# The mask additions of one batch moved from VectorE to GpSimd, with every engine's list of work laid out anew

## The reference, cut to what matters

```
h = relu(layernorm(x))
q, k, v = h @ Wq.T + bq, h @ Wk.T + bk, h @ Wv.T + bv         # 4 heads of 32
s = clip(q @ k.T / sqrt(32), -10, 10); s = where(adj == 0, -10, s)
attn = softmax over each of 8 chunks of 128 columns apart
x = x + layernorm(sum over chunks(attn @ v) @ Wo.T + bo + h) * gamma + beta

h = relu(layernorm(x)); Wh = h @ W
e = leaky_relu(Wh @ a1 [row] + Wh @ a2 [column], 0.2)          # 1024 x 1024
e = where(adj > 0 or i == j, e, -inf)
x = x + elu(softmax(e) @ Wh)
```

## Time and profile before

| | |
|---|---|
| median of 3 runs | 709.34 us (707.78 to 710.83) |
| the profiled execution | 708.66 us, its span 706.9 us |
| DVE busy | 662.2 us (94%), 1165 instructions |
| ACT busy | 649.4 us (92%), 1140 |
| PE busy | 647.7 us (92%), 4393 |
| POOL busy | 523.0 us (74%), 629 |

### The profile page before, as it was taken

One profiled execution on the slowest core, in us unless ns is written; L12 is line 12 of the kernel. 1 busy time (PEld: TensorE's weight loads), 2 busy tenths in 40 slices (PEclk: granted clock), 3 DMA queues, 4 the chain that ended last, 5 costly groups with the idle time before them and its releaser, 6 DMA issues. The chain is left out here.

```text
span 706.9 us, 13598 instructions
## 1 busy us (share of the span) xinstructions
PE 647.7 (92%) x4393; PEld 348.3 (49%) x4393; DVE 662.2 (94%) x1165; ACT 649.4 (92%) x1140; POOL 523.0 (74%) x629
## 2 busy tenths in 40 slices
PE   3689999999899999999999999999999999995976
PEld 1433443343355554547455554556436463564865
DVE  1899999999999999999999999999999999999875
ACT  2799999998999999999999989999999989997665
POOL 2144585663779888898889768988879778889864
PEclk9999999999999999999999999999999999998899
DMA  8742133224211233233223143122232213010111
GB/s 285 245 155 105 68 128 120 96 83 150 90 52 62 98 120 120 84 112 109 72 76 125 63 150 112 60 76 105 83 112 98 69 46 106 16 46 30 54 52 47
DMA packets 58647, 68.53 MB, mean 97 GB/s; under 512 B 5328, under 2 KB 35024, under 8 KB 58576
## 3 DMA queue, kind: packets, MB, share of 16 engines
q1 hardware_dynamic: 57568, 67.39, 28.1%
q10 hardware_dynamic: 1008, 0.26, 0.2%
HBM read 21.50 MB, written 12.58 MB: 48 GB/s over the span
## 5 line engine op out<-in xcount | busy, mean ns | idle before, releaser
L1452 DVE SCALAR_TENSOR_TENSOR probs<-score,cap 128x1024 f32<-128x1024 f32 x256 | 305.5, 1212 | 5.6 <-ACT score L1297 4.4
L1297 ACT ACTIVATE score<-score 128x1024 f32<-128x1024 f32 x256 | 259.9, 1028 | 10.7 <-PE score L1644 9.9
L1644 PE MATMUL score<-query_stack,key_stack 128*128 128x512 f32 x512 | 186.4, 451 | 18.9 <-DVE probs L1452 17.2
L1224 POOL TENSOR_TENSOR gathered<-gathered,scaled 128x512 f32<-128x512 f32 x112 | 154.4, 1379 | 53.5 <-DVE scaled L1478 52.6
L1249 POOL TENSOR_TENSOR ring<-ring,see_t 128x512 f32<-128x512 f32 x112 | 133.1, 1200 | 17.7 <-DVE ring L1543 17.5
L1644 PEld LDWEIGHTS score<-query_stack,key_stack 128*128 128x128 f32 x512 | 79.5, 189 | 131.8 <-DVE probs L1452 100.4
L1661 PE MATMUL work<-probs,ones 128*32 128x512 f32 x1024 | 135.2, 602 | 0.1
L1655 PE MATMUL work<-probs,value 128*32 128x512 f32 x1024 | 132.8, 598 | 0.1
L1727 PEld LDWEIGHTS work<-wh,ring 128*128 128x128 f32 x896 | 107.2, 194 | 17.8 <-issue 7.6
L1727 PE MATMUL work<-wh,ring 128*128 128x130 f32 x896 | 110.5, 280 | 4.4 <-ACT ring L1365 4.3
L1365 ACT ACTIVATE ring<-ring,wh 128x512 f32<-128x512 f32 x128 | 90.2, 735 | 5.9 <-POOL ring L1249 3.9
(11 more groups left out here) (117 smaller groups left out, 836.8 us busy)
## 6 DMA issues: line engine op xcount, KB each, us to landing
query_stack<-parts SPq DMA_DIRECT2D x64, 256.0 KB, 2.9
key_stack<-parts SPq DMA_DIRECT2D x56, 256.0 KB, 2.5
x_in<-in_x SPq DMA_DIRECT2D x16, 256.0 KB, 2.9
h_kept<-x_in SPq DMA_DIRECT2D x16, 256.0 KB, 2.2
res<-h_kept SPq DMA_DIRECT2D x16, 256.0 KB, 2.7
h<-in_x SPq DMA_DIRECT2D x16, 256.0 KB, 3.2
x_kept<-res SPq DMA_DIRECT2D x16, 256.0 KB, 2.2
gat_x<-x_kept SPq DMA_DIRECT2D x32, 128.0 KB, 2.2
```

Source lines behind the costliest of these rows:

```text
L1224: nc.gpsimd.tensor_tensor(sums, sums, scaled[:, k % SCALED], ALU.add).then_inc(gathered_step, 1)
L1297: nc.scalar.activation(some, some, ACT.Exp, scale=DH ** -0.5).then_inc(exp_done, 1)
L1452: nc.vector.scalar_tensor_tensor(out=probs[:, group_of(b, k) % KEPT], in0=score[:, h:h + GROUP, :], scalar=LOW, in1=caps.broadcast_to([P, ...
L1644: last = nc.tensor.matmul(score[:, head, :], key_stack[:, head, chunk * P:(chunk + 1) * P], query_stack[:, head, half * HALF:(half + 1) * ...
```

## The change

In the table VECTOR, batch 6 loses its eight `hide` steps (the odd tiles); in GPSIMD all sixteen have a place. Batch 7 keeps half and half, batches 0 to 5 were POOL's before and stay so. All five tables and BANKS have new numbers throughout. The code that walks them is untouched; its lines stand five lower in the new file, since a table became shorter.

```diff
 VECTOR = {
     0: {
...
-        "bias_row": [1092],
...
+        "bias_row": [2829],
...
     6: {
...
-        "hide": [None, 4986, None, 5120, None, 5253, None, 5386, None, 5714, None, 6120, None, 6188, None, 6256],
...
 GPSIMD = {
...
     6: {
...
-        "hide": [4818, None, 4933, None, 5047, None, 5162, None, 5566, None, 5915, None, 6112, None, 6226],
...
+        "hide": [5500, 5614, 5875, 6119, 6234, 6348, 6463, 6577, 6692, 6991, 7106, 7220, 7335, 7449, 7564, 7678],
...
 SYNC = {
     0: {
...
-        "store_h": [920, 1992],
-        "load_residual": [1190, 2365],
...
+        "store_h": [1250, 2320],
...
+        "load_residual": [2225, 5283],
```

More of the change, by code:

```diff
@@ L49 @@
         "turn_x": [932, 1794],
[L50 to L66, removed]
-    },
-    1: {
[L69 to L83, removed]
-    },
@@ L85 @@
-    2: {
[L86 to L103, removed]
-    },
@@ L105 @@
-    3: {
[L106 to L123, removed]
-    },
@@ L185 @@
[L185 to L203 removed]
+        "mask": [1132, 1284, 1485, 1949, 2027, 2167, 2413, 3230],
@@ new lines @@
+        "see": [1130, 1236, 1326, 1858, 2100, 2134, 7222, 7796],
+        "cast": [1164, 1370, 2040, 2464],
+        "key": [1430, 2963],
+        "edges": [1496, 1710, 1892, 2168, 2316, 3635, 5033, 5407],
+        "query": [1644, 3283],
+        "probs": [2525, 2638, 2850, 3057, 3170, 3409, 3522, 3783, 3896, 4147, 4366, 4480, 4718, 4920, 5181, 5294,
+            5615, 5728, 5979, 6152, 6353, 6484, 6717, 6908, 7109, 7256, 7435, 7683, 7830, 8026, 8276, 8418],
+        "bias_row": [2829],
+        "gather": [3349, 4010, 4593, 4832, 5555, 5842, 6092, 6265, 6597, 7021, 7548, 7943, 8139, 8597, 8770, 9286],
@@ L680 @@
[L680 to L693 removed]
+        "beta": [2630, 8343],
@@ new lines @@
+    3: {
+        "rstd_x": [-19410, -18182],
+        "gather": [None, -4158, -4016, -3213, -2795, -2650, -1812, -1569, None, 223, 365, 608, 977, 1434, 1679,
+            2257],
+        "residual": [-1326, 2664],
+        "beta": [1220, 2385],
+        "rstd_y": [2072, 6671],
+        "gamma": [2517, 7341],
+        "x1": [2984, 7501],
+        "rstd_z": [4291, 7990],
+        "row_shift": [12157],
+        "hide": [12998, 13113, 13227, 13342, 13468, 13847, 14306, 14549, 15109, 15245, 15917, 16530, 16773, 16980,
+            17095, 17605],
+        "add_x1": [15707, 17523, 19536, 19649],
+        "add_below": [16887, 19038, 19731, 23336],
+    },
@@ new lines @@
+    7: {
+        "rstd_x": [-23736, -21191],
+        "gather": [None, -10590, -10448, -10052, -9445, -9202, -8866, -8605, None, -7690, -7203, -6786, -6314,
+            -5661, -5315, -4818],
+        "residual": [-9695, -5532],
+        "beta": [-8738, -6092],
+        "rstd_y": [-5846, -4285],
+        "gamma": [-5186, -3871],
+        "x1": [-4947, -3610],
+        "rstd_z": [-4470, -2794],
+        "row_shift": [-737],
+        "hide": [-302, None, -170, None, 42, None, 336, None, 467, None, 679, None, 910, None, 1122],
+        "add_x1": [1025, 1334],
+        "add_below": [1237, 1429],
```

1159 lines of the change are left out of this document (593 added, 566 removed).

## The result

The changed kernel takes 703.21 us in the median (702.33 to 704.53, 4 runs), the kernel before 709.33 beside it (707.78 to 710.83, 4 runs). The ratio is 0.9912, with a 95% interval of 0.9895 to 0.993. It is faster by 6.1 us; 704.8 was predicted. The profiled execution took 702.33 us with a span of 700.6, which is 6.3 less than the span of 706.9 before.

A forecast was written before the change was run, and what follows sets the result against it. DVE, ACT and PE together were taken to bound the middle, with open time at both ends. 708.66 - 7.4 (start) - 0.8 (middle) + 4.0 (end) = 704.5 us, or 705.1 from the median; 704.8 was predicted, range 698 to 711.

The forecast's parts named there:

- The start: Up to the first `probs`: bias_row later and stacks issued earlier bring it 7.4 us forward, with 4.6 and 8.9 as ends.
- the end: First leaky of batch 6 to first of batch 7: eight more hides on POOL delay the shares, 4.0 us dearer.
- The middle: From 50 us to the last `probs`: two DVE instructions leave this stretch, 0.8 us won, with 4 us to either side.
- the last stretch: The last 27.1 us, from the first leaky of batch 7: same work, so 0, with 1 us to either side.
- behind the last `probs`: After the last `probs`, DVE busy only 15.77 of 17.88 us: a leaky and an invert of batch 5 cost nothing there.
- the rest of the new order: In the middle: can win at most the 11.5 us of idle time; given 0 with 4 us to either side.
- The peaks of batch 7: In the end: said to finish before the last share, so row_shift still waits for the copies of wh.
- The free end: Rival: the end costs 1 us or nothing; 701.5 us, or 698 if the middle loses 3 us idle; chance 0.25.
- The loads: Rival: stacks crawl behind set-up loads, or mask tiles wait; first `probs` at 30 us, 708.5 us, no change; chance 0.17.
- The stalled middle: Rival: new lists add waits in the middle, deciding from 8 us more idle; with 10 more 714.5 us; chance 0.13.
- The rule of twice the time on POOL: Skill's advice for POOL's elementwise work: a hide 1.32 us instead of 1.17, the end 1.2 us dearer, 705.7 us; not adopted.
- a clash with leaky: In the end: if DVE's leaky held POOL up, eight hides would cost 1.5 us more and the sum be 706.

The follow-up runs named there:

- e1: The kernel before with bias_row alone moved back on PE (with its bank) and DVE: 706.8 us, ratio 0.996.
- e2: The kernel before with bias_row moved back and load_residual of batch 0 put behind both stacks on SP: 702.9 us, ratio 0.99.
- e9: The kernel before with POOL's wide sums except the hides cut to 16 columns per row (output not the layer's): 696.85 us, ratio 0.9829.
- e6: e3 with gamma and x1 of batch 7 later on POOL and DVE's stats_z and moments_z of batch 7 earlier: 702.43 us, ratio 0.9901.
- e4: The kernel before with all sixteen hides of batch 6 on POOL and nothing else changed: 714.0 us, ratio 1.0058.
- e3: The changed kernel with the eight odd hides of batch 6 given back to DVE: 705.88 us, ratio 0.9945.
- e8: e6 with 48 unread transposes added in PE's wait ahead of the first share: 702.27 us, ratio 0.9894.
- e7: The changed kernel with 88 unread transposes added in PE's wait ahead of the first share: 701.54 us, ratio 0.988.

## Why the prediction was right, step by step

The sum was 2.1 us too high against the profiled execution (4.2 us to be won, 6.3 won), and it was that close partly by luck. The start came as worked out, 0.4 us short, and the end 0.5 better. The middle and the last stretch gave 3.1 us that the working didn't have, and the way behind the last `probs` took 1.1 back.

**The start**: -7.4 predicted, -6.97 measured. Each mark holds: `see` at 10.83 (11), key_stack at 16.04 (16), bias_row later without a wait, the first `probs` at 27.67 (27.2, between 25.7 and 30). The working named the full queue of DMAs as the second brake and put the end of the stacks at 25.5. The first scores did wait for the second stack, and started at 25.77:

```profile
25.77 1.21 PE L1639 MATMUL score<-query_stack,key_stack 128*128 128x512 f32 x4 [0.97 <-DMA query_stack<-parts]
```

e1 and e2 show that bias_row alone isn't enough and that both moves together are.

**The middle**: -0.8 with 4 to either side, -2.84 measured. This is the term that was mis-sized. The leaky and the invert left the stretch with 0.9 us, but bias_row and half a key came in from the start (1.0) and a cast went there (0.7); the working counted these three at the start and not here. And "the rest of the new order" was costed as idle time alone, with DVE's work held fixed. The work changed: the peaks got 3.2 us shorter, by meeting POOL's sums less (rows above, e9). So the last `probs` came 9.8 us earlier, where some 8 was the mark. The clash could be seen before, in a mean of 1.47 us for 48 peaks whose undisturbed ones take 1.21.

**Behind the last `probs`**: "there they cost nothing" was wrong by 1.09 us. DVE has the room (16.41 busy of 18.97 us), so the two may well cost nothing; but PE sets this stretch, as its last product of wh releases ACT's copy and with it POOL's row_shift. From the last `probs` to the end of that product PE works without a gap in both, for 14.20 us before (626.45 to 640.65) and 14.92 after (616.64 to 631.56). It has as many share products there as before, but 36 matmuls for context and row sums of the chunked attention instead of 24 (4.7 us instead of 3.0), while a turn_hidden of 0.7 us went. The other 0.4 us lie behind it. The working looked at DVE alone there.

**The end**: +4.0 predicted, +3.47 measured. The first share comes 14.01 us after the first leaky (14.7 predicted), since POOL's hides follow each other every 1.12 us where 1.17, the duration of one, was taken for each, and gamma and x1 take 1.28 and not 1.39. PE's wait and the slow shares are there, two at 2.94 us where 2.72 was taken. Nothing behind made it up: the last share ends 33.94 us after the first leaky, 3.69 later than before. That the size came out doesn't show that the hides cost it: e6 has the eight back on DVE and an end of 38.04.

One step of the working was misread and did no harm. The peaks of batch 7 don't end before the last share. In the kernel before, the last one ends at 676.69, 2.1 us behind that share and 0.1 behind ACT's last copy of wh (676.58):

```profile
675.47 1.22 DVE L1522 CUSTOM_DVE_ANT_0 near_row<-score,see 128x1024 f32<-128x1024 f32 x1
```

In the changed kernel the peaks end 1.1 us behind the last share (669.46 + 1.22), and the copies at 671.34, so row_shift still waits for the copies, as the working had it, and 5.03 us lie between the last share and the next leaky where 5.2 was taken.

**The last stretch**: 0 predicted with 1 to either side, -1.05 measured; its cause is open.

**The rivals.** The free end: no, the end cost 3.47, and e4, with the hides alone moved, is 4.2 us slower. The loads: they were the brake that the sum named, but did not crawl; the rival's 708.5 also leaves out the 0.8 us of the middle, with which its steps give 707.3 to 707.9. The stalled middle: idle time rose by 1.2 us, far from the 8 from which it decides. The rule of twice the time on POOL would have made a hide 1.32 us; the sixteen of batch 6 take 1.15 to 1.17 each, and 1.60 at most beside DVE's in e3. The 1.5 us that a clash with leaky would have cost did not come: fourteen leaky run beside the first nine hides of the changed kernel, which take no longer for it. The sentence of the Trainium skill that the prediction leans on there, in Advanced Engine Details and Errata, Mode Summary, speaks of VectorE's 2p instructions alone, a condition that the prediction left out.

## What to carry to other kernels

A change of this kind is several changes: measure each alone before you credit any. Here two steps moved at the start win 7 us in the old lists, and the move that gives the change its name costs 4 there; in the new lists, taking it back with its neighbours adapted makes no difference that can be told from the noise. When lists are laid out anew, look beside idle time for instructions whose mean lies well above their fastest, and ask what runs on the other engine next to the slow ones.

## What the runs showed of the hardware

- DVE and POOL hold each other up in some forms of DVE's instructions. Of those with two tiles in SBUF, the peaks take 1.21 us alone and 1.58 beside POOL's wide sums, 2.32 at worst, and the hides 0.66 alone and up to 1.64. Without most of POOL's sums 8.5 us of the middle go (e9). The Trainium skill's GPSIMD Engine Reference, section 8 Key points, names this case, DVE instructions with two SBUF inputs, and SBUF — State Buffer, section Terms, says that the loser blocks for the whole instruction; the rows at 145.43 and 146.60 agree.
- It isn't two inputs alone. The steps `see` and `edges` of the masks read one bf16 tile of SBUF and take 0.42 us alone; in the kernel before, those at 25.79 and 26.54 take 0.84 and 1.49, each until 0.3 us behind the end of a wide sum of POOL that had started first (24.73 to 26.34 and 26.30 to 27.74):

```profile
25.79 0.84 DVE L1587 TENSOR_SCALAR see<-ring 128x1024 bf16<-128x1024 bf16 x1
26.54 1.49 DVE L1594 TENSOR_SCALAR ring<-ring 128x1024 bf16<-128x1024 bf16 x1
```

- `probs`, leaky and the normalising product, which read one operand from PSUM, keep 1.21, 0.74 and 0.68 us beside POOL's wide sums and without them, and so do the statistics, which read one f32 tile of SBUF, with 0.28.
- Shares took 2.94 us each behind a wait of PE of 10.93 us, with the granted clock at 0.62, 3.27 behind one of 3.98 in e8, and 1.90 behind one of 1.39 in e7, with the clock at 1.00.
- A DMA issue that waits holds up the issues behind it on SP. In e1 SP stood at load_residual for 8.1 us (12.99 to 21.08) with the stacks behind it; with load_residual behind the stacks, the first `probs` came 3.5 us earlier (32.47 to 28.98).
